# Scan stage: wider rows for h and B, and ten instead of nine of the 24 products with B on GpSimd

## The reference

```python
def _selective_scan(xs, dts, A, Bs, Cs):      # xs, dts: b k d l; A: k d n; Bs, Cs: b k n l
    def step(h_prev, t):
        x_t, dt_t, B_t, C_t = t
        dA = jnp.exp(dt_t[..., None] * A)
        dBx = (dt_t * x_t)[..., None] * B_t[:, :, None, :]
        h = dA * h_prev + dBx
        y = jnp.einsum('bkdn,bkn->bkd', h, C_t)
        return (h, y)
    ...
    h0 = jnp.zeros((b, k, d, n), xs.dtype)
    _, ys = jax.lax.scan(step, h0, seq)
```

## Time and profile before

| | |
|---|---|
| median of 3 runs | 20604.83 us (20602.19 to 20609.28) |
| profiled execution | 20604.12 us, of which the span of the trace is 20602.3 us |
| busy share of the span | DVE 89%, POOL 78%, PE 73%, ACT 50% |
| scan stage | from about 6157 us to about 19922 us of the span |
| DMA | 2520.51 MB, 122 GB/s over the span |

### The profile page before, as it was taken

How to read it: one execution, slowest core, us unless ns; L and a number is a source line. 1 busy time by engine, 2 the same in 40 slices (tenths; PEclk the granted TensorE clock), 3 DMA queues, 4 the chain that set the end, 5 groups by cost and what they waited for, 6 DMA issues and landing times. The chain is left out here.

```text
span 20602.3 us, 287674 instructions
## 1 busy us (share of the span) xinstructions
PE 15096.4 (73%) x82072; PEld 5460.7 (27%) x82072; DVE 18321.8 (89%) x20601; ACT 10241.1 (50%) x19687; POOL 16030.5 (78%) x6484
## 2 busy tenths in 40 slices
PE   8999999987766667666666666666666666676652
PEld 5555555542221111111111111111111111111112
DVE  5555555579989999999999999999999999999986
ACT  4444444457764444444444444444444444444443
POOL 0000000049989999999999999999999999999988
PEclk9999999998877777777777777777777777777765
DMA  0000000047776666666666666666666666666668
GB/s 22 18 18 18 18 18 18 18 135 249 252 235 129 136 130 140 133 136 134 131 139 133 138 132 133 137 133 140 131 135 135 134 138 130 137 133 136 137 145 230
DMA packets 1091855, 2520.51 MB, mean 122 GB/s; under 512 B 247606, under 2 KB 398648, under 8 KB 1075328
## 3 DMA queue, kind: packets, MB, share of 16 engines
q1 hardware_dynamic: 1090688, 2508.11, 54.5%
HBM read 2000.43 MB, written 507.38 MB: 122 GB/s over the span
## 5 line engine op out<-in xcount | busy, mean ns | idle before, releaser
L1254 POOL TENSOR_TENSOR c_pr<-c_hs,c_c_u 128x1568 f32<-128x1568 f32 x3072 | 9908.8, 3236 | 13.4 <-DVE c_hs L1218 12.9
L1152 ACT ACTIVATE c_psum<-c_dt_u,c_a_neg 128x784 f32<-128x784 f32 x6144 | 5641.4, 918 | 6991.1 <-DVE c_hs L1218 6937.0
L1084 PE MATMUL c_psum<-c_pr,c_red 128*64 128x392 f32 x24576 | 6829.8, 679 | 5.9 <-POOL c_pr L1254 5.9
L1218 DVE TENSOR_TENSOR_SCAN c_hs<-c_psum,c_dbx 128x785 f32<-128x785 f32 (+1 forms) x3840 | 6737.2, 1770 | 20.7 <-issue 20.7
L1073 PE MATMUL c_psum<-c_br_u,c_sel 48*128 48x512 bf16 (+1 forms) x7680 | 2596.8, 430 | 4293.5 <-DVE c_dbx L1195 4191.0
L1218 DVE TENSOR_TENSOR_SCAN c_hs<-c_psum,c_dbp 128x785 f32<-128x785 f32 (+1 forms) x2304 | 4104.9, 1782 | 11.4 <-ACT c_psum L1152 11.4
L1243 POOL TENSOR_TENSOR c_dbp<-c_u_u,c_bp_u 128x784 f32<-128x784 f32 x2304 | 3943.0, 1711 | 127.8 <-DVE c_hs L1218 76.3
L1195 DVE TENSOR_TENSOR c_dbx<-c_u_u,c_psum 128x784 f32<-128x784 f32 x3840 | 3621.8, 943 | 39.9 <-PE c_psum L1073 39.9
L196 POOL TENSOR_TENSOR a_xpb<-a_x_sb,a_pb_sb 98x768 f32<-98x768 f32 x128 | 231.3, 1807 | 4064.9 <-DVE a_x L285 4050.8
L1084 PEld LDWEIGHTS c_psum<-c_pr,c_red 128*64 128x64 f32 x24576 | 1809.7, 174 | 3396.5 <-issue 3126.2
L1073 PEld LDWEIGHTS c_psum<-c_br_u,c_sel 48*128 48x128 bf16 x7680 | 459.8, 101 | 7885.7 <-DVE c_dbx L1195 6879.7
(11 more groups left out here) (131 smaller groups left out, 18323.4 us busy)
## 6 DMA issues: line engine op xcount, KB each, us to landing
c_c_u<-scr_bc SPq DMA_DIRECT2D x512, 1568.0 KB, 29.0
c_dt_u<-scr_dt SPq DMA_DIRECT2D x512, 588.0 KB, 7.3
c_u_u<-scr_u SPq DMA_DIRECT2D x512, 588.0 KB, 11.2
c_bp_u<-scr_bc SPq DMA_DIRECT2D x512, 588.0 KB, 22.2
scr_dt<-p_dt_o SPq DMA_DIRECT2D x384, 392.0 KB, 3.4
scr_u<-p_u_o SPq DMA_DIRECT2D x384, 392.0 KB, 2.8
scr_y<-c_y_sb SPq DMA_DIRECT2D x256, 294.0 KB, 19.2
d_yin<-scr_y SPq DMA_DIRECT2D x32, 2352.0 KB, 14.5
```

The source lines that it names most:

```text
L1084: mm = pe.matmul(Y(3 * w + q)[64 * h:64 * h + 64, :], red[:], pr[:, s % RP, HT * h:HT * h + HT], start=(p == 0 and opens(w)), stop=(p == N ...
L1152: nc.scalar.activation(dA(s)[:, data], dt_u[:, d, s // NPR, :], ACT.Exp, scale=a_neg[:, k, s:s + 1]).then_inc(exp_done, 1)
L1218: nc.vector.tensor_tensor_scan(hs[:, s % RH, way], dA(s)[:, way], added, 0.0, ALU.mult, ALU.add).then_inc(scan_done, 1)
L1254: nc.gpsimd.tensor_tensor(pr[:, s % RP:s % RP + 2, :], hs[:, s % RH:s % RH + 2, data], c_u[:, d, s % NPR:s % NPR + 2, :], ALU.mult).then_i ...
```

## The change

The rows of `hs` and `bp_u` become 788 columns wide instead of 786. The data stay in columns 1 to 784. `bp_u` gets a fourth row in each half, for the pair of states 1, and `POOL_STEPS` goes from 9 to 10 steps of the 24: 9 and 17 come in, 13 goes out. `dbx` and `dbp` keep rows of 786.

```diff
-POOL_PAIRS = (3, 5, 7)
-POOL_STEPS = (3, 5, 7, 11, 13, 15, 19, 21, 23)
+POOL_PAIRS = (1, 3, 5, 7)
+POOL_STEPS = (3, 5, 7, 9, 11, 15, 17, 19, 21, 23)
 DVE_STEPS = tuple(s for s in range(3 * NPR) if s not in POOL_STEPS)
...
-        bp_u = sb("bp_u", [128, 2, len(POOL_PAIRS), CT + 2])
+        bp_u = sb("bp_u", [128, 2, len(POOL_PAIRS), CT + 4])
         br_u = sb("br_u", [3 * NS, 2, CT], BF16)
         dbx = sb("dbx", [128, RB, CT + 2])
         dbp = sb("dbp", [128, RG, CT + 2])
-        hs = sb("hs", [128, RH, CT + 2])
+        hs = sb("hs", [128, RH, CT + 4])
...
-                                 rows(32 * d)[:, h, POOL_PAIRS[0]::2, :].to_broadcast([64, 3, CT])).then_inc(u_in[d], 16)
+                                 rows(32 * d)[:, h, POOL_PAIRS[0]::2, :].to_broadcast([64, len(POOL_PAIRS), CT])).then_inc(u_in[d], 16)
```

## The result

The changed kernel takes 21398.78 us (median of 4 runs, 21397.24 to 21402.12) against 20604.68 us for the kernel before: a ratio of 1.0386, with a 95% interval of 1.0369 to 1.0402. The forecast was 20387 us: the measured time lies 1012 us above it, and on the other side of the kernel before. The rival in which the products with C become slow gave about 21450 us.

A forecast was written before the change was run, and what follows sets the result against it. DVE was taken as the bound, at 53.74 us a unit, falling to 52.89. 256 x (0.86 - 0.01) = 217 us off the span of 20602.3, plus 1.8 around it, gave 20387 us, range 20350 to 20430.

The forecast's parts named there:

- rival in which the products with C become slow: POOL: distance of second operand behind first counts, products with C take 3.48 us to next start; about 21450 us; chance 0.12.
- part on the products with C: POOL's products with C, reading two hs rows against c_u, go from 3.24 to 2.96 us with both rows at 4.
- reading with pairs of elements: POOL loses time when both operands enter new 16-byte pieces within the same two elements: 0 and 12 slow, 4 quick.
- The bounds: POOL's product with C: 2.96 us if both halves are quick, 3.52 us if both are slow.
- The rival's sum: POOL with slow products with C: 12 x 3.48 + 15.3 = 57.1 us a unit, 3.3 over 53.74, times 256.
- DVE: Scan stage: DVE sets the pace; one product fewer takes its unit from 53.74 to 52.89 us; row width costs nothing.
- the product's price: DVE's one product given up per unit: 256 x (0.86 - 0.01) = 217 us saved.
- POOL in time: POOL's products come before DVE's scans need them, with 2.5 us a unit to spare.
- Loads hidden: The larger bp_u load lands about 39 us after its start, needed at 48.7 us: hidden, about 10 us to spare.
- The rival with no change: POOL's products with C stay at 3.24 us, POOL needs 53.7 us a unit: 20590 us; chance 0.04.
- No address counts: POOL's two product lengths stay whatever the starts; ten products with B make 55.1 us a unit: 20950 us; chance 0.01.

The follow-up runs named there:

- e5: The kernel before with only the rows of bp_u made 788 wide, still nine products with B on POOL: 20596.62 us, ratio 0.9998.
- e7: e1 with nine products with B on POOL, using the steps and three bp_u rows of the kernel before: 20589.82 us, ratio 0.9995.
- e9: e1 with a fifth slot of y_sb, giving chunk 0 of the column orders its own place: 20373.6 us, ratio 0.9889.
- e1: The exchanged kernel: the changed kernel with the operands of POOL's product with C exchanged, c_u first, hs second: 20435.24 us, ratio 0.9919.
- e3: The kernel before with only the rows of hs made 788 wide: 21322.49 us, ratio 1.035.
- e6: The changed kernel with the rows of hs back at 786: 20661.72 us, ratio 1.0029.
- e2: The changed kernel with the data of hs two columns further on, rows starting at 12, operands in old order: 20436.51 us, ratio 0.992.
- the map: The changed kernel plus 31 POOL products of 128 x 768 with varied operand and output starts, other engines idle: 21451.08 us (one run).
- e10: e1 with the fifth slot of y_sb and an eleventh product with B (step 13) on POOL: 20142.7 us, ratio 0.9777.

## Why the prediction was wrong

**The step that failed** is in the part on the products with C: "By the reading with pairs of elements it makes no difference which operand is off, and both rows at 4 are quick. I take 2.96". It does make a difference. With `hs` at 4 as the first operand and `c_u` at 0 as the second, the distance is -4, that is 12, and slow; the quick row of each pair was the one at 12, and the new width did away with it. The measured value is 3506 ns over all 3072, against a bound of 3.52 us for two slow halves. The bounds were right, and the choice between them rested on a mechanism that three observations, all with the first operand at 0, could not tell from its rival. The trace had no row with the first operand off, and the prediction said so, but still gave the rival 0.12. A sign that three points leave open is nearer to even chances.

**The rival's sum** was close in every term: 57.1 us a unit forecast, 56.8 measured, and 21450 us against 21399. What is left is 3.455 in place of 3.48 us to the next start, 0.3 us a unit.

**DVE.** That DVE set the pace before was right: quicker products with B alone (e5) and a POOL with 4.6 us less work a unit (e7) bring no change that can be measured. That a unit becomes 52.9 us was right for the kernel without the waits for ACT: (2648 + 1892) / 24 = 189.2 units in 10000 us in e9, 52.86 us each. e7 against e9 gives the product's price, 216 us. The row width cost DVE nothing that shows there.

**POOL in time.** Right: in the exchanged kernel DVE waits for POOL 2.3 us in 10000, and POOL waits for scans (464.7 + 31.8) / 188.4 = 2.6 us a unit, where 2.5 were forecast.

**Loads hidden.** Half right. Past the stage's first unit POOL doesn't wait for a load. But the load stands in front of the stores in SP's queue, and I asked only who waits for the load. The waits behind the stores had no term in the sum and cost 62 us in the exchanged kernel (e1 against e9). That is not all the larger load's doing: ACT waited for stores 55.0 us in 10000 before, 98.3 in e1, and 133.8 in e3 with the small load. How the 62 us divide between the load's size and its start was not measured.

**The rival with no change** was built in e6: POOL at 53.7 us a unit and DVE at 52.9 should have left 20590 us and gave 20662. Its waits point to the stores and to two engines with little to spare against each other; no run separates the two.

**No address counts** is excluded by e1, e2, e5 and the map.

## What to carry to other kernels

Before padding a row for alignment, write down for each two-input GpSimd instruction where both operands start modulo 16 bytes and take the difference with its sign; exchanging the factors is free and turns a difference of 12 into 4, or back. A difference of 8 bytes is quick in either order, and one of 0 slow in either. An instruction over two rows averages over two starts, so its length alone can't tell which row is the quick one: measure the two apart before both are made alike. And when a load grows or starts later, ask not only who waits for it but which DMA is issued behind it, and what stands in the queue of the engine that waits for that.

## What was not expected of the hardware

The rule of the map above, with its sign: GpSimd's product of two float32 operands takes 2962 ns for 1568 columns and 1546 for 768 where the difference is 4, which is (2962 - 1546) / 800 = 1.77 ns a column; where it is 12 (or 0), 3506 and 1803 ns, 2.13 a column, a fifth more. At 8 the 768 columns take 1546 ns too. Why the sign counts is a guess: if the engine takes first and second elements by turns, then at differences of 0 and 12 the second operand steps into its next 16 bytes one or three turns behind the first, and at 8 and 4 five or seven turns behind. No run here tests that order of turns.

An instruction's length in the trace can grow without costing time. In e7 the scans have a mean of 1841 and 1853 ns and the products with B 1014 ns, against 1770, 1782 and 943 in the earlier trace rows, and the units are as long as before (53.7 us). The groups, 8000 to 18000 us, of e7, and then POOL's of e10:

```profile
L1218 DVE TENSOR_TENSOR_SCAN c_hs<-c_psum,c_dbx 128x785 f32<-128x785 f32 (+1 forms) x2794 | 5059.2, 1841 | 18.2 <-issue 18.2
...
L1218 DVE TENSOR_TENSOR_SCAN c_hs<-c_psum,c_dbp 128x785 f32<-128x785 f32 (+1 forms) x1675 | 3103.4, 1853 | 0.0
L1195 DVE TENSOR_TENSOR c_dbx<-c_u_u,c_psum 128x784 f32<-128x784 f32 x2793 | 2831.2, 1014 | 0.0
...
L1261 POOL TENSOR_TENSOR c_pr<-c_c_u,c_hs 128x1568 f32<-128x1568 f32 x2311 | 6994.8, 3037 | 0.0
...
L1250 POOL TENSOR_TENSOR c_dbp<-c_u_u,c_bp_u 128x784 f32<-128x784 f32 x2117 | 3489.2, 1648 | 10.5 <-DVE c_hs L1225 10.5
```

In e10 POOL's products are 3037 and 1648 ns long in place of the 2962 and 1574 of e1, and yet a unit takes 10000 / (2311 / 12) = 51.9 us, which is 12 x 2.92 + 11 x 1.53. No run shows where the longer readings come from. The count of scans or products in a stretch is the safer measure of its pace.
